# Chased graph stages: scattering the parked sums from where they lie

## What is computed

```python
h = relu(layernorm(x)); x = x + L0(h)      # relation-typed messages, summed by dst
h = relu(layernorm(x)); x = x + L1(h)      # attention, summed by src
h = relu(layernorm(x)); x = x + L2(h)      # two rounds of mean over neighbours:
#   msg = h[src]; s = segment_sum(msg, dst); mean = s / max(count, 1)
#   h = layernorm(h @ W_self.T + mean @ W_neigh.T + b)
h = relu(layernorm(x)); x = x + L3(h)      # GCN: segment_sum(x_proj[src] * norm, dst)
```

## Time and profile before

| | us |
|---|---|
| median of 3 runs | 3703.67 (3701.21 to 3707.44) |
| the profiled execution | 3701.02 |
| its span, first to last instruction | 3699.3 |
| ... SAGE0, scatters of POOL | 2182.4 to 2477.8 |
| ... SAGE1, scatters of POOL | 2761.2 to 3084.9 |
| ... GCN, scatters of POOL | 3394.0 to 3674.6 |

### The profile page before, as it was taken

The page is one execution under the profiler, slowest core; times in us unless marked ns, Lnnn a source line. Parts: engine busy times, 40 slices in busy tenths (PEclk is TensorE's granted clock), DMA queues, the critical chain, the costliest instruction groups (busy, mean ns, idle before and its releaser), DMA issues. The chain is left out here.

```text
span 3699.3 us, 82926 instructions
## 1 busy us (share of the span) xinstructions
PE 2617.9 (71%) x19724; PEld 2288.0 (62%) x19724; DVE 2511.4 (68%) x11513; ACT 1948.6 (53%) x5393; POOL 2612.2 (71%) x2673
## 2 busy tenths in 40 slices
PE   3899998888466666630018887767888775887888
PEld 3899997666465555530007765546776665776777
DVE  5677776889555445538864448883448887665998
ACT  1333334777454444421117777763446664776777
POOL 3677773666788888855457778767778784777876
PEclk9999999999787777765559999998999998999999
DMA  7544444888433333339972239982229997222998
GB/s 277 215 149 140 147 147 136 268 267 269 125 42 41 41 41 41 41 50 317 311 229 53 52 109 297 294 287 67 52 60 332 335 337 246 53 52 79 309 311 287
DMA packets 336597, 638.73 MB, mean 173 GB/s; under 512 B 62000, under 2 KB 90832, under 8 KB 335208
## 3 DMA queue, kind: packets, MB, share of 16 engines
q1 hardware_dynamic: 241758, 502.00, 41.0%
q0 software_dynamic: 90944, 133.85, 16.3%
q10 hardware_dynamic: 3786, 1.65, 0.2%
HBM read 371.35 MB, written 277.50 MB: 175 GB/s over the span
## 5 line engine op out<-in xcount | busy, mean ns | idle before, releaser
L750 POOL DMA_INDIRECT got<-rows,gidx x588 | 606.3, 1031 | 225.8 <-issue 173.3
L797 POOL DMA_INDIRECT sums<-got,sidx x588 | 614.9, 1046 | 168.7 <-issue 156.5
L1056 ACT ACTIVATE n_h<-ring 128x128 f32<-128x128 f32 x1176 | 482.7, 482 | 56.5 <-DVE ring L1730 45.8
L971 ACT ACTIVATE psum_out<-bank 128x132 f32<-128x132 f32 x784 | 218.8, 279 | 531.4 <-PE bank L1223 530.7
L1324 PE MATMUL bank<-ring,ident 128*128 128x128 f32 x2352 | 459.3, 277 | 0.0
L1204 PE MATMUL bank<-parked 128*128 128x128 f32 x3136 | 388.7, 278 | 11.9 <-DVE parked L1558 11.9
L1189 PE MATMUL bank<-ident,e_h 128*128 128x128 f32 x588 | 96.0, 287 | 408.0 <-ACT e_h L934 408.0
L1204 PEld LDWEIGHTS bank<-parked 128*128 128x128 f32 x3136 | 371.5, 194 | 13.7 <-issue 8.6
L811 POOL DMA_INDIRECT attsums<-ring,sidx x196 | 312.3, 1594 | 80.2 <-issue 64.5
L1324 PEld LDWEIGHTS bank<-ring,ident 128*128 128x128 f32 x2352 | 361.6, 194 | 0.0
L1461 DVE COPY gidx<-src_i 128x4 int32 (+1 forms) x227 | 45.2, 199 | 465.2 <-DMA got<-rows,gidx 204.4
(11 more groups left out here) (183 smaller groups left out, 7250.7 us busy)
## 6 DMA issues: line engine op xcount, KB each, us to landing
ring<-sums SPq DMA_DIRECT2D x392, 264.0 KB
ring<-rows SPq DMA_DIRECT2D x392, 264.0 KB, 4.7
rows<-ring SPq DMA_DIRECT2D x294, 264.0 KB
attsums<-parked SPq DMA_DIRECT2D x49, 528.0 KB
rows<-parked SPq DMA_DIRECT2D x49, 528.0 KB
ring<-attsums SPq DMA_DIRECT2D x98, 264.0 KB
rowsg<-ring SPq DMA_DIRECT2D x98, 264.0 KB
ring<-rowsg SPq DMA_DIRECT2D x98, 264.0 KB
```

What stands on the lines that cost most here:

```text
L750: pool.indirect_dma_start(out=got[:, b, j, 0:width], out_offset=None, in_=table[:, :], in_offset=bass.IndirectOffsetOnAxis(ap=gidx[:, b, j ...
L797: pool.indirect_dma_start(out=sums[:, :], out_offset=bass.IndirectOffsetOnAxis(ap=sidx[:, b, j:j + 1], axis=0), in_=got[:, b, j, :], in_of ...
L1056: last = nc.scalar.activation(n_h[:, b, k, :], x_data(phase, g)[:, k, :], ACT.Relu, bias=x_col(phase, g, k, COL_C), scale=x_col(phase, g, ...
```

## The change

`copy_parked` and `scatter_copied` are replaced by one function, which issues the four DMAs of a round from `parked` with the row numbers in `last_i`. The rounds are no longer a hardware loop: they are written out, 196 scatters with constant addresses in each of the three stages. `round_landed` now uses constants and is called two rounds behind, ahead of the scatters of round r. The semaphore `lent` goes. The wait for the last gathered rows ahead of the scatters stays.

```diff
-                def copy_parked(r):
-                    b = r.mod(GOT)
-                    if r.i is not None or r.offset >= 3:
-                        round_landed(r.back(3))
-                    nc.gpsimd.tensor_copy(sidx[:, b, :], last_i[:, bass.ds(r.scaled(TPR), TPR)])
-                    pool.wait_ge(parked_ready.sem, parked_ready.after(r, parked_before(phase)))
-                    gate(pool)
-                    nc.gpsimd.tensor_copy(got[:, b, :, :], parked[:, bass.ds(r.scaled(TPR), TPR), :])\
-                        .then_inc(lent.sem, 1)
-
-                def scatter_copied(r):
-                    b = r.mod(GOT)
-                    if r.i is None and r.offset == ROUNDS - 1:
-                        round_landed(r.back(2))
-                    pool.wait_ge(lent.sem, lent.after(r, parked_before(phase)))
+                def scatter_parked(r):
+                    pool.wait_ge(parked_ready.sem, parked_before(phase) + r + 1)
                     gate(pool)
                     for j in range(TPR):
+                        t = r * TPR + j
                         pool.indirect_dma_start(
-                            out=sums[:, :], out_offset=bass.IndirectOffsetOnAxis(ap=sidx[:, b, j:j + 1], axis=0),
-                            in_=got[:, b, j, :], in_offset=None,
-                            bounds_check=bound, oob_is_err=False).then_inc(scattered[r.mod(2)].sem, 16)
+                            out=sums[:, :], out_offset=bass.IndirectOffsetOnAxis(ap=last_i[:, t:t + 1], axis=0),
+                            in_=parked[:, t, :], in_offset=None,
+                            bounds_check=bound, oob_is_err=False).then_inc(scattered[r % 2].sem, 16)
...
-                    run_steps(pool, [(copy_parked, 0), (scatter_copied, 1)], ROUNDS, GOT, behind=2)
-                    for r in range(ROUNDS - 2, ROUNDS):
-                        b = r % 2
-                        pool.wait_ge(scattered[b].sem, (parity_first(seg_index(phase), b) + r // 2 + 1) * 16 * TPR)
-                        pool.sem_inc(rounds_landed.sem, 1)
+                    for r in range(ROUNDS + 2):
+                        if r >= 2:
+                            round_landed(r - 2)
+                        if r < ROUNDS:
+                            scatter_parked(r)
```

More of the change, by code:

```diff
@@ L354, in gnn_stack_kernel @@
         counts_taken = Signal(sem("counts_taken"), 1, 2)
-        lent = Signal(sem("lent"), 1)
         rounds_landed = Signal(sem("rounds_landed"), 1, 1)
@@ L775, in round_landed @@
                 def round_landed(r):
-                    b = r.mod(2)
-                    pool.wait_ge(scattered[b].sem, scattered[b].after(r.div(2), parity_first(seg_index(phase), b)))
+                    b = r % 2
+                    pool.wait_ge(scattered[b].sem, (parity_first(seg_index(phase), b) + r // 2 + 1) * 16 * TPR)
                     pool.sem_inc(rounds_landed.sem, 1)
-                def copy_parked(r):
-                    b = r.mod(GOT)
-                    if r.i is not None or r.offset >= 3:
-                        round_landed(r.back(3))
-                    nc.gpsimd.tensor_copy(sidx[:, b, :], last_i[:, bass.ds(r.scaled(TPR), TPR)])
-                    pool.wait_ge(parked_ready.sem, parked_ready.after(r, parked_before(phase)))
-                    gate(pool)
-                    nc.gpsimd.tensor_copy(got[:, b, :, :], parked[:, bass.ds(r.scaled(TPR), TPR), :])\
-                        .then_inc(lent.sem, 1)
-                def scatter_copied(r):
-                    b = r.mod(GOT)
-                    if r.i is None and r.offset == ROUNDS - 1:
-                        round_landed(r.back(2))
-                    pool.wait_ge(lent.sem, lent.after(r, parked_before(phase)))
+                def scatter_parked(r):
+                    pool.wait_ge(parked_ready.sem, parked_before(phase) + r + 1)
                     gate(pool)
                     for j in range(TPR):
+                        t = r * TPR + j
                         pool.indirect_dma_start(
-                            out=sums[:, :], out_offset=bass.IndirectOffsetOnAxis(ap=sidx[:, b, j:j + 1], axis=0),
-                            in_=got[:, b, j, :], in_offset=None,
-                            bounds_check=bound, oob_is_err=False).then_inc(scattered[r.mod(2)].sem, 16)
+                            out=sums[:, :], out_offset=bass.IndirectOffsetOnAxis(ap=last_i[:, t:t + 1], axis=0),
+                            in_=parked[:, t, :], in_offset=None,
+                            bounds_check=bound, oob_is_err=False).then_inc(scattered[r % 2].sem, 16)
                 def add_pair(r, q):
```

## The result

| | us |
|---|---|
| before, median of 5 runs | 3703.7 (3698.3 to 3708.4) |
| after, median of 5 runs | 3682.2 (3674.7 to 3687.7) |
| ratio of the runs | 0.9942, 95% interval 0.9932 to 0.9953 |
| profiled execution of after (span) | 3674.7 (3673.0) |

The change saves 21.5 us by the medians, 0.6%. The profiled execution of after is the fastest of its five, so the traces show 26.3 us between them; a part of that is the choice of the execution, not the change.

What follows compares the result with a forecast made beforehand. It took GpSimd's pace to hold SAGE0, transfers SAGE1, and ScalarE and TensorE's loop nearly GCN. Gains of 12 + 4 + 2 = 18 us from 3703.7 gave 3686 us, range 3670 to 3699.

Steps and rivals of the forecast that it cites:

- What bounds each stage: SAGE0 held by GpSimd, then ScalarE and TensorE's loop, floor 279.4 us; GCN near that floor; SAGE1 at its transfers.
- the chain of waits: In SAGE1, from 2750 to 3060, issue and landings of GpSimd's scatters make up 94% of the profile's chain.
- A round on GpSimd, 5.73 to 5.11 us: Each scatter round loses 0.62 us without copies, 30.4 us a stage; scatters span about 265, 294 and 250 us.
- SAGE0, 12 us: SAGE0's node loop falls from 295.7 us towards GCN's 284.1; gain 12 us, ends 0 and 16.
- SAGE1, 4 us: SAGE1 gains 4 us from its start and from VectorE's line 1819 no longer running beside copies, at most 11 us.
- the beginning: SAGE1 up to 2840, before its queues are full, where GpSimd can give some us.
- GCN, 2 us: GCN gains 2 us, ends 0 and 5, mostly at its start, where two pairs of copies go, 1.9 us at most.
- Announcing and straight code at nothing: On GpSimd, announcing rounds costs nothing, 1 us a round without cover; written-out code nothing, at worst 15 us a stage.
- Hidden anyway: Rival, chance 0.17: late loads hold the node loops, or scatters from `parked` cost more; 3699 us.
- slower: Rival, chance 0.05: denser scatters take bandwidth from node loads, 5 us a stage; 3719 us, 3712 in part.
- near the floor: Rival, chance 0.12: all stages near their floors, gaining SAGE0 16, GCN 5, SAGE1 10 us; 3673 us.
- POOL the bound in SAGE1: Rival, chance 0.05: GpSimd bounds SAGE1 too, so its 30 us come in full; 51 us in all, 3653 us.

Runs made afterwards that it cites:

- with_copy_2: Changed kernel with each round's two copies put back as idle work whose result nobody reads: 3695.0 us, against 3705.6 for the kernel before on that chip, ratio 0.9979.
- copy_late: with_copy_2 plus two fills ahead of each stage's first scatters, starting them 1.1 to 1.3 us later: 3706.8 us, against 3702.7 for the kernel before, ratio 1.001.

## Why the prediction was right, point by point

The median of 3682.2 us is 3.8 us under the forecast of 3686 and inside the range; the gain of 21.5 us stands against 18. Under the total, the steps fared differently, and that the 12 us of SAGE0 came out is in part luck.

- *What bounds each stage.* Right for SAGE0 and GCN: the loop of ScalarE and TensorE took over at once, 280.8 and 282.6 us against a floor of 279.4. Right for SAGE1 against the chain of waits: GpSimd went through it 41 us faster and only 5 to 9 us came out of it.
- *A round on GpSimd, 5.73 to 5.11 us.* Right where nothing collides: GCN's 196 scatters span 252.2 us, with 250 forecast. (The 0.62 us are less than the two copies because these overlap each other by 0.1 us and stand in the place of a gap between scatters, not because one lies beside a scatter.) Wrong in SAGE0: 278.7 us for 265. The step took GCN's durations for SAGE0; every second scatter there meets line 1786 and takes 1.30 us. The miss cost nothing in time.
- *SAGE0, 12 us.* 14.9 in the trace, 12.2 when timed alone. The size was right, the reason was not complete. The prediction held the 0.62 us of a round responsible; with the copies at their full length 285.0 us were reached all the same. It read POOL's pace as 5.73 us a round, but SAGE0's 295.4 us are 6.07 us a round on average, and it did not ask where the rest comes from: from rounds that VectorE's line 1799 stretches. The second step that failed is the start: two pairs of copies ahead of the first scatter were counted for GCN alone, at 1.9 us at most, and passed one for one. In SAGE0 a start 1.2 us later made a difference of some 10 us.
- *SAGE1, 4 us.* 5.1 when timed alone, 9.1 in the two traces. Both terms were there, the beginning and VectorE's time beside the copies. Of the second the cause holds: line 1819 fell from 742 to 660 ns in the mean, and fills did not raise it; what the beginning gave wasn't timed by itself. "The same bytes need the same time" at a DMA share of 0.99 was too strict: the same 300 us moved 333 GB/s before and 345 after, 3% more.
- *GCN, 2 us.* 1.5 in the trace, 2.7 when timed alone, with an interval that includes nothing.
- *Announcing and straight code at nothing.* No time shows up in either. In the three stages of the changed kernel GpSimd's idle times that a landing ends are 0.31 us on average, where 0.30 is usual between scatters, and of with_copy_2 and copy_late, both in straight code, one has the old kernel's time. The stall of round 28 was also there before, so it is none of written-out code.
- *The rivals.* Hidden anyway, 3699 us, slower, 3712 to 3719, near the floor, 3673, and POOL the bound in SAGE1, 3653, are all excluded by the interval (3678.5 to 3686.3 us); SAGE1 alone gave 5.1 us and not 30. What the denser scatters take from the loads is not seen in the time: SAGE0's DMA share rose to 0.95 only.

## What to carry to other kernels

Where one loop chases another at nearly the same pace, look at the lead as well as at the pace: here 1.2 us of delay ahead of the first step cost 10 us over 98 steps, because the late loop met more of another engine's work and lost its pace. The start is the cheapest thing to change. Judge the gain of an engine by the stage and by who waits for it (27.0 us of SyncE's waits in SAGE0, 0.9 in most of SAGE1), not by its removed work, 138 us here for 21 gained, nor by a chain of waits that stays on an engine because that engine never idles. When work is put back to test a cause, put it back in its full length and also move the start by itself, or two causes are taken for one.

## What the runs showed of the hardware

- A GpSimd scatter that starts in the first half microsecond of VectorE's line 1786 (two SBUF inputs, 0.67 us) takes longer. In the changed kernel's SAGE0 83 of 196 do, with a median of 1.30 us; of the other 113 none takes over 1.1 us. The later it starts in that line, the less it loses. Over SAGE0 in ten traces (line 1799 in some) the mean is 1.36 us for a start 0.1 to 0.2 us into the line, 1.29 for 0.2 to 0.3, 1.17 for 0.3 to 0.4 and 0.99 for 0.5 to 0.6, as if the scatter waited for the line to end. Line 1772, as long (0.69 us) but with one of its inputs in PSUM, does nothing of the kind: the four scatters of the changed kernel's SAGE0 that start under it alone take 0.97 to 0.98 us, and 23 in the kernel before at most 1.00. In GCN, where no operation of this length with two SBUF inputs runs, the median stays at 0.97. The page "SBUF — State Buffer" of the Trainium skill (section "Who interferes with whom", practical consequences) infers the opposite for such an operation, that it takes only the read interface while the writing of descriptors needs the other; the measured rows decide. These scatters also take their row numbers from SBUF (`last_i`, `sidx`), so it may be this read that waits and not the writing of descriptors; no run separates the two.
- GpSimd stalls for 2.0 to 4.8 us before the second scatter of round 28 in each of the three stages, in all ten traces that were not taken on the slow chip: before and after the change, in loop and straight code, with and without copies (3.16 and 3.69 us in SAGE0). From one such stall to the next there are 392 indirect DMAs. It would fit something that fills up after a count of DMAs; no experiment changed the count, and the cause is not shown.
- One chip of those met ran the kernel before in 4731 us instead of 3703. In the kernels traced there GpSimd's scatters have their usual length, and single waits between engines take 16 us and more, many of them while GpSimd scatters. The mean granted clock is 0.80 to 0.81 in them, against 0.89 to 0.90 on the other chips; which is cause and which is effect is not shown.
